# Key stores on GpSimd's queue, and four steps moved at the seam of two stages, in a graph attention kernel

## What is computed

```python
row_zero = x.sum(-1) == 0
q_exp = jnp.where(row_zero[..., None], 0.0, q[:, None, :])
self_feat = jnp.concatenate([x, q_exp], -1) @ W_self.T + b_self
output = self_feat
for d in range(2):
    A = adj if d == 0 else swapaxes(adj, 1, 2)       # [B, N, N, 11]
    A = A[:, :, :20, :]
    kv = self_feat[:, :20]                            # 20 keys for each of 128 batches
    qh, kh = heads(self_feat @ Wq[d].T + bq[d]), heads(kv @ Wk[d].T + bk[d])
    aff = einsum(qh, kh) / sqrt(dh) + mask(A) + (A @ w_bias + b_bias)
    w = softmax(aff, -1)
    output += heads_out(einsum(w, kv), Wout[d]) + bout[d]
out = x + relu(output)
```

## Time and profile before

| | us |
|---|---|
| median of 3 runs | 1888.92 |
| lowest and highest | 1884.96, 1889.0 |
| the profiled execution, whole time | 1889.68 |
| its span | 1887.9 |
| TensorE busy | 1790.1 (95%) |
| VectorE, ScalarE, GpSimd busy | 1117.5, 953.2, 773.0 |

### The profile page before, as it was taken

One profiled execution on the slowest core, in us unless ns is written; L12 is line 12 of the kernel. 1 busy time (PEld: TensorE's weight loads), 2 busy tenths in 40 slices (PEclk: granted clock), 3 DMA queues, 4 the chain that ended last, 5 costly groups with the idle time before them and its releaser, 6 DMA issues.

```text
span 1887.9 us, 45438 instructions
## 1 busy us (share of the span) xinstructions
PE 1790.1 (95%) x14792; PEld 1629.0 (86%) x14792; DVE 1117.5 (59%) x1879; ACT 953.2 (50%) x1655; POOL 773.0 (41%) x689
## 2 busy tenths in 40 slices
PE   8998778886999999999999999999999999999997
PEld 5898778885898999889899989999988989998886
DVE  2555455566666566666666666656666666666532
ACT  2333233333555555655555655555565555566543
POOL 0433333320344444444444444444444444444444
PEclk9998888997999999999999999999999999999999
DMA  7122222336555656555665655565755565565431
GB/s 213 37 77 77 72 71 76 82 101 138 142 148 150 185 147 173 148 147 154 166 170 148 165 147 149 146 185 134 189 149 147 148 168 169 147 172 148 122 99 61
DMA packets 291524, 258.16 MB, mean 137 GB/s; under 512 B 105968, under 2 KB 221936, under 8 KB 291312
## 3 DMA queue, kind: packets, MB, share of 16 engines
q1 hardware_dynamic: 287136, 255.46, 50.2%
q10 hardware_dynamic: 4176, 0.02, 0.1%
HBM read 199.25 MB, written 56.10 MB: 135 GB/s over the span
## 4 chain that ended last, share of the span: by engine, by line
PE 77%; issue 7%; SPq 7%; DVE 3%; POOL 3%; DMA 2%; ACT 1%; POOLq 0%; DVEq 0%; ACTq 0%
PE bank L1647 30%; PE bank L1662 20%; PE low_banks L1623 9%; PE bank L1683 9%; PE bank L1675 4%; SPq L663 4%; PE bank L1650 2%; PE bank L486 1%; POOL kv_prod L799 1%; SPq L70 1%; SPq L669 1%; DMA k_dram<-kv_kst 1%; PE bank L1691 1%; DVE kv_pt L717 1%; DVE kv_vt L756 1%
## 5 line engine op out<-in xcount | busy, mean ns | idle before, releaser
L1647 PE MATMUL bank<-kx,xt_main 128*128 128x160 f32 x4096 | 632.7, 303 | 0.0
L1647 PEld LDWEIGHTS bank<-kx,xt_main 128*128 128x128 f32 x4096 | 581.5, 192 | 6.0 <-issue 0.3
L1488 POOL TENSOR_TENSOR res<-res,xk 128x512 f32<-128x512 f32 x128 | 163.8, 1280 | 451.1 <-ACT res L1527 451.1
L1545 ACT ACTIVATE wtt<-bank 128x384 f32<-128x384 f32 (+1 forms) x256 | 109.6, 428 | 439.4 <-PE bank L1675 439.4
L1384 DVE TENSOR_TENSOR sc<-bank,masks 128x320 f32<-128x320 f32 x256 | 125.6, 491 | 341.9 <-PE bank L1650 340.1
L1532 ACT ACTIVATE kx<-low_banks 128x1920 f32<-128x1920 f32 (+5 forms) x201 | 306.2, 1524 | 43.1 <-PE low_banks L1623 43.0
L1470 POOL TENSOR_TENSOR sc<-sc,mx 128x640 f32<-128x640 f32 x128 | 160.0, 1271 | 310.5 <-DVE mx L1396 310.5
L1662 PE MATMUL bank<-ws_h,xh_main 128*128 128x512 f32 x512 | 217.7, 425 | 3.5 <-DVE res L1410 3.4
L1623 PE MATMUL low_banks<-key_tile,a_rows 32*128 32x160 f32 (+3 forms) x4288 | 202.5, 315 | 7.6 <-ACT kx L1532 4.0
L1662 PE MATMUL bank<-ws_l,xh_main 128*128 128x512 f32 x512 | 202.8, 396 | 0.0
L1662 PE MATMUL bank<-ws_h,xl_main 128*128 128x512 f32 x512 | 202.6, 396 | 0.0
(11 more groups left out here) (145 smaller groups left out, 3051.4 us busy)
## 6 DMA issues: line engine op xcount, KB each, us to landing
rows_main<-in_x SPq DMA_DIRECT2D x256, 128.0 KB, 4.6
xs<-in_x SPq DMA_DIRECT2D x64, 512.0 KB, 4.7
xk<-in_x SPq DMA_DIRECT2D x64, 512.0 KB, 3.7
res<-c_dram SPq DMA_DIRECT2D x64, 512.0 KB, 5.5
out<-res SPq DMA_DIRECT2D x128, 256.0 KB, 3.3
adj<-in_mask_BxSxSx_ik SPq DMA_DIRECT2D x32, 440.0 KB, 6.1
adj<-in_mask_BxSxSx_ik SPq DMA_DIRECT2D x128, 110.0 KB
vbd<-v_dram SPq DMA_DIRECT2D x768, 10.0 KB
```

Source lines behind the costliest of these rows:

```text
L1488: pool.tensor_tensor(res[:, p.par, b, :], res[:, p.par, b, :], xk[:, p.par, b, :], ALU.add).then_inc(res_ready, 1)
L1647: mm = nc.tensor.matmul(dst, xt[:, j, p.ring + b, :], kx[:, t.par, :, 2 * j:2 * j + 2, w * NG:w * NG + NG] .rearrange("p r c m -> p c r m" ...
```

## The change

1. The key stores leave SP. GpSimd issues the store of key p itself, inside `by_conditions`, after the wait for `kv_out` and ahead of the wait for `p_turned` and its product.
2. `late_loads` stands ahead of the value stores of half 7 (there are no key stores on SP now).
3. `early_turn` is cut in two. The turn of the first x pair goes to the end of half 6, behind `turn_constants(6)`; the mask's part (`early_mask`) stays where it was in half 7.
4. New `first_loads` on SP, between the value stores and the `z_dram` stores of half 7: the second edges and the second rows for sums, which the window loop's slot issued before.
5. The tile `zc` is cleared by GpSimd at the start of its window program, with a semaphore of its own, instead of by VectorE.

The diff, without the lines that only pass names along:

```diff
--- before.py
+++ after.py
@@ -646,22 +646,19 @@
                 for s in k_stored:
                     sp.wait_ge(s, 16 * C)
                 v["early_loads"](sp)
-            for p in range(NK):
-                if last and p == 2:
-
-                    sp.wait_ge(pe_feat, C * HALVES)
-                    sp.wait_ge(f_low, C * HALVES)
-                    v["late_loads"](sp)
-
-                sp.wait_ge(kv_out, 2 * NK * n + p + 1)
-                sp.dma_start(v["k_dram"][p, :, bass.ds(n * HB, HB), :],
-                             kst[:, p % 2, :].rearrange("p (b m) -> p b m", m=NG)).then_inc(k_stored[p % 2], 16)
+            if last:
+
+                sp.wait_ge(pe_feat, C * HALVES)
+                sp.wait_ge(f_low, C * HALVES)
+                v["late_loads"](sp)
             for m in range(NK):
                 d, c = m // C, m % C
                 sp.wait_ge(v_turned, NK * n + m + 1)
                 for k in range(NQ):
                     sp.dma_start(v["v_dram"][NQ * c + k, d, :, bass.ds(n * HB, HB), :],
                                  vt[Q * k:Q * k + NG, m % 4]).then_inc(v_stored[m % 4], 16)
+            if last:
+                v["first_loads"](sp)
             sp.wait_ge(z_turned, n + 1)
             for r in range(NQ):
                 for e in range(2):
...
@@ -742,11 +739,7 @@
             if not tail:
                 turn_x(blk + 1, n + 2, par)
             if last:
-
-                dve.wait_ge(pe_feat, C * HALVES)
-                dve.wait_ge(x_low, C * HALVES)
-                dve.wait_ge(f_low, C * HALVES)
-                v["early_turn"](dve)
+                v["early_mask"](dve)
             for m in range(NK):
 
                 dve.wait_ge(kv_out, 2 * NK * n + NK + m + 1)
...
@@ -757,6 +750,11 @@
                 if m < 2:
                     constant_sums(n, 6 + m)
             turn_constants(n)
+            if tail and not last:
+
+                dve.wait_ge(pe_feat, C * HALVES)
+                dve.wait_ge(x_low, C * HALVES)
+                v["early_turn"](dve)
 
         nonzero(0, 0)
         dve.wait_ge(v["ct_out"], 1)
...
@@ -794,6 +792,8 @@
         def by_conditions(n, p):
 
             pool.wait_ge(kv_out, 2 * NK * n + p + 1)
+            pool.dma_start(v["k_dram"][p, :, bass.ds(n * HB, HB), :],
+                           kst[:, p % 2, :].rearrange("p (b m) -> p b m", m=NG)).then_inc(k_stored[p % 2], 16)
             if due(NK * n + p - 1):
                 pool.wait_ge(p_turned, NK * n + p - 1)
             pool.tensor_tensor(prod[:, p % 2, 1, :].rearrange("p (b m) -> p b m", m=NG),
...
@@ -1057,6 +1057,7 @@
     edge_consts = sem("edge_consts")
     set_once = sem("set_once")
     cleared = sem("cleared")
+    zc_cleared = sem("zc_cleared")
     x_turned = sem("x_turned")
     x_high = sem("x_high")
     x_low = sem("x_low")
...
@@ -1271,9 +1272,18 @@
     def early_turn(dve):
         dve.wait_ge(rows_loaded[0], 16 * NQ)
         turn_pair(dve, Pair(0, 0), range(C))
+
+    def early_mask(dve):
         dve.wait_ge(edge_consts, 32)
         count_and_weigh(dve, 0, 0)
         total_and_mask(dve, 0, 0)
+
+    def first_loads(sp):
+
+        sp.wait_ge(bias_sum[0], 1)
+        load_edges(sp, 1, 0)
+        sp.wait_ge(summed, 2)
+        load_sum_rows(sp, Pair(0, 1))
 
     def load_constants(sp, p):
 
...
@@ -1304,7 +1314,7 @@
                 if t.back(4).real():
                     sp.wait_ge(pe_s, scored(t.back(1), 3))
                 elif t.n == 0:
-                    sp.wait_ge(set_once, 2)
+                    sp.wait_ge(zc_cleared, 1)
                 load_constants(sp, t)
             if has_window(n) and due(t.n + 1):
 
...
@@ -1324,8 +1334,9 @@
                 g = edge_group(t.back(-1))
                 if has_edges(g) and due(g):
 
-                    sp.wait_ge(bias_sum[0], g)
-                    load_edges(sp, g, 0)
+                    if not isinstance(g, int) or g > 1:
+                        sp.wait_ge(bias_sum[0], g)
+                        load_edges(sp, g, 0)
             if done.real():
                 store(done, 0)
             if due4.real():
...
@@ -1346,7 +1357,7 @@
                     sp.wait_ge(res_ready, 2 * (due4.n - 1))
                 sp.dma_start(xk[:, due4.par],
                              v["x"][bass.ds(2 * due4.n, 2)].rearrange("b n f -> n b f")).then_inc(xk_loaded[due4.par], 16)
-            if n.real() and due(n.n):
+            if n.real() and due(n.n - 1):
 
                 sp.wait_ge(summed, 2 * n.n)
                 load_sum_rows(sp, n)
...
@@ -1363,9 +1374,8 @@
             sp.wait_ge(s, 32 * (PAIRS // 2))
 
     def vector_program(dve):
-        nc.vector.memset(zc[:].bitcast(F32), 0.0).then_inc(set_once, 1)
         nc.vector.memset(nzm[:], 0.0).then_inc(set_once, 1)
-        dve.wait_ge(set_once, 2)
+        dve.wait_ge(set_once, 1)
         for b in range(2):
             for o in (0, 2):
                 nc.vector.memset(nzm[:, b::2, ZK * b + o:ZK * b + o + 1], 1.0).then_inc(set_once, 1)
...
@@ -1443,7 +1453,7 @@
             if has_edges(g) and (due(g) or t.c % 2):
                 total_and_mask(dve, g, t.c % 2)
 
-        dve.wait_ge(set_once, 6)
+        dve.wait_ge(set_once, 5)
         slots(dve, slot, -1)
 
     def s_bank(t, a):
...
@@ -1451,6 +1461,8 @@
         return bank[4 + n][:, 0:2 * UN]
 
     def gpsimd_program(pool):
+        pool.wait_ge(v["kv_out"], 4 * DIRS * C * v["KBLOCKS"])
+        pool.memset(zc[:].bitcast(F32), 0.0).then_inc(zc_cleared, 1)
         for s in v["k_stored"]:
             pool.wait_ge(s, 16 * DIRS * C * v["KBLOCKS"])
         for s in v["v_stored"]:
```

4 lines of the change are left out of this document (2 added, 2 removed).

## The result

The changed kernel takes 1820.38 us (median of 4 runs, 1817.72 to 1824.19) where the kernel before takes 1887.42 in the same comparison: a ratio of 0.9647, with a 95% interval of 0.9623 to 0.9672. That is 67.0 us or 3.5% faster, at the forecast of 1816 within 4.4 us and inside its range. The profiled execution took 1818.22 us, its span is 1816.2, and the span before was 1887.9: 71.7 us less.

The account below looks back on a forecast made before the run. Key stores queued behind SP's other transfers held the halves above TensorE's pace. Halves at 36.5 us give 58.7 and the seam 14.5, together 73.2 us off the profiled 1889.68; with the median 0.76 lower, 1816 us, range 1811 to 1845.

Parts of the forecast that it names:

- g: Time GpSimd takes to issue one key store; unknown before, chosen near 0.97 us.
- S: Time from a key store's issue on GpSimd to its landing, taken as g + 1.47 us.
- the ring: Half's chain of keys, GpSimd's stores and landings: 25.15 + 3(g + S), 35.4 us, hidden under TensorE's 36.26 by 0.9.
- 2g + 5.45: Time from key 0 of a half until store 2 goes out, behind two issues, two products and the conditions.
- S + 2.4: One step from a key store's issue to the next, for stores 3 to 5, each waiting for a landing.
- g + 12.5: From store 5 to the next half's key 0: issue, product, x turn, then value transposes.
- the sum's term: Seam path through the second rows for sums: out at 35.05, first scores at 44.3 us, a gain of 15.3.
- A: The forecast itself: halves at TensorE's pace, up to 37 us, giving 1813 to 1819 us; chance 0.62.
- B: Halves: the ring through GpSimd takes over, 39.8 us a half and 1839 us at g = 1.7; chance 0.25.
- C: Halves: only SP's issue time is saved, 2.7 us a half, giving 1856 us; chance 0.04.
- D: Halves: slower, GpSimd's issue as dear as ScalarE's longest, 3.98 us; 53.4 us a half, 1934 us; chance 0.05.
- E: Seam: another input of the first scores comes as late as before; only 58.7 us gained, 1830 us; chance 0.04.

Follow-up runs that it names:

- The stores alone: Changed kernel with only the key stores moved to GpSimd; x turn, first loads and clearing of zc put back as before: 1824.18 us, ratio 0.9670.
- The store behind the product: Changed kernel with GpSimd issuing each key store after its own product of the same tile instead of ahead of it: 1829.71 us, ratio 0.9699.
- three stores for one: Changed kernel with GpSimd issuing two extra scratch stores ahead of each key store, ScalarE waiting for all three: 1879.67 us, ratio 0.9956.

## Why the prediction was right, point by point

**The bound.** Right. What held the halves was the place of the key stores behind SyncE's other transfers. The stores alone gave 58.2 us in the halves, and eight more issues a half on SyncE cost 0.3 of their 3.2 us there. The forecast took TensorE's pace from half 0, which ran without gaps, so the 11 us that the clock gave back are in its sum, though it does not name them.

**The halves: right in the sum, by two errors.** Forecast 36.5, measured 36.61 a half, though not even: 35.19 to 38.65. The price of GpSimd's issue was too high:

```profile
L795 POOL DMA_DIRECT2D k_dram<-kv_kst x64: 580/580/710, 81.0 to 351.5; - x64
```

g is 0.58 us at the least and at the median, not 0.97. The landing was 2.3 at the median (2.1 to 6.5), where S = g + 1.47 with g = 0.97 had given 2.44. With these, 25.15 + 3(g + S) is 33.8, and the halves should all have been hidden under TensorE's 36.26. Half 3, of 38.65 us, shows what the ring really was. Its first piece, key 0 to store 2, was 9.02 us, where 2g + 5.45 gives 6.61; in halves 0 to 2 and 4 to 6 it was 6.91 to 7.91. The step that failed is the conditions' place in the row:

```profile
195.95 3.09 POOL L776 TENSOR_TENSOR kv_rc<-kv_nz,kv_cbb 128x320 f32<-128x320 bf16 x4 [2.20 <-DVE kv_cbb L676]
```

GpSimd's conditions wait for VectorE, which the row of before that I had used did not the earlier trace rows, and store 2 stands behind them. That row is of half 1; in halves 2 to 5 of the kernel before the same instruction waited 0.62 to 1.96 us for VectorE. The next steps were 4.98, 4.82 and 5.15 us, the S + 2.4 of the prediction with an S of 2.4 to 2.8. From store 5 to the next key 0 were 14.68, where g + 12.5 gives 13.08; in five of the other six halves it was 13.11 to 13.14, as worked out. Behind both long pieces of half 3 stand SyncE's value stores, for which VectorE waits before it can use a slot of `vt` again:

```profile
193.99 0.71 DVE L749 STREAM_TRANSPOSE kv_vt<-kv_vst 128x512 f32<-128x512 f32 x1 [2.57 <-DMA v_dram<-kv_vt]
...
227.12 0.71 DVE L749 STREAM_TRANSPOSE kv_vt<-kv_vst 128x512 f32<-128x512 f32 x1 [1.08 <-DMA v_dram<-kv_vt]
```

The first is the last value transpose of half 2, and VectorE makes the conditions' inputs only behind it, from 195.22; the second is the last but one of half 3, just ahead of key 0 of half 4. So the ring passes TensorE's pace in half 3, and in halves 4 and 5, of 35.19 and 35.68, it is 0.7 to 1.2 us below it.

TensorE lost nothing by this. Its last matmuls for key 0 of halves 3 and 4 are

```profile
188.53 0.31 PE L933 MATMUL low_banks<-kv_fh,wkv_l 128*128 128x320 f32 x1
...
224.90 0.31 PE L933 MATMUL low_banks<-kv_fh,wkv_l 128*128 128x320 f32 x1
```

36.37 us apart, and it is the same, within 0.01, from each half to the next from half 1 to half 7; in the window from 116 to 336 us TensorE is busy for 220.00 of 220.00. The 38.65 are ScalarE falling behind by 2.3 us more, which the six banks took up. So the 1.9 us that the kernel with ScalarE's stores has less in its halves (254.42 for 256.29) are nearly all ScalarE's lag of 1.8 us at key 0 of half 7, and not time of TensorE. TensorE's pace of 36.26 a half was right to 0.1.

**ScalarE's wait: a miss that cost the halves nothing.** The wait for landings fell from 130.0 us to 81.3 in 28 waits, not to under 25. Such a row is in each step of the ring:

```profile
206.40 0.53 ACT L853 ACTIVATE kv_kst<-low_banks,bk_s 128x320 f32<-128x320 f32 x1 [3.34 <-DMA k_dram<-kv_kst]
```

I had counted only what a landing would add beyond the step. But in a ring in which ScalarE works 1.5 us of a step of 4.8, it waits some 3.3 for whatever is last, and the landing became that in place of the product. TensorE waited 0.6 us for it in all, against 52.1 before, so the wait was on the side with slack. The wait said how near the ring was, not what it cost. What a shorter ring is worth shows at the seam: with ScalarE's own stores halves and seam together are 296.4 us and not 300.6.

**SyncE.** Right. It stands idle from 211.48, the end of its x loads, to 220.45, 9 us, within half 3, and 9.7 to 14.3 us in each of halves 1, 2 and 4 to 6.

**The seam: the number right, partly by luck.** Forecast 44.3, measured 44.31. From key 0 of half 7: VectorE began its sums at 5.6 (forecast 5.0), the mask at 16.36 (16.6), the value stores at 21.05 (21.3), the sum rows went out at 34.85 (35.05). The mask was forecast to wait for its edges. They were issued at 11.75 and not at 10.5, but landed 4.0 us later and not 6.1, at 15.8, and the mask's start was the end of VectorE's sums, which had been put at 15.3: two errors that cancel to 0.2 us. The z stores landed 3.30 us behind their last issue, not 1.6, so at 41.7 and not 40.0:

```profile
374.52 3.30 DMA z_dram<-kv_zt
```

The constants' loads then landed 2.5 behind their issue at 377.89, near the short end that was allowed, and they, not the sum rows, were the last for the first scores, by the 0.41 us of the row above. The chain of the sum rows ended at 43.9; the forecast's 9.26 from their issue to the first scores was itself 0.2 too long, since the first scores of before start at 453.82 in the timeline and not at 454.03. So the sum's term was the second to last, and the two paths ended within half a microsecond of each other. The gain is 15.1, where 14.5 was taken and 9.8 to 15.3 was the range. Of it 8.7 come with the stores alone.

**The early turn, and the clearing.** The prediction had the turn's 2.1 us hidden. The kernel that undoes it is 2.8 us longer in the seam and 0.9 to 2.3 in the median, with a late landing of the edges in the trace, so this stays open, as told above. Clearing the tile was said to cost nothing on GpSimd, and it doesn't; that it would have cost 1.3 to 1.8 us if left on VectorE was not worked out.

**The sum.** Forecast 73.2 less in the span, measured 71.7: halves 57.95 for 58.7, seam 15.1 for 14.5, less 1.3 before and behind, which is spread. The medians differ by 67.0: the profiled execution of the kernel before took 2.3 us more than its median, that of the changed kernel 2.2 less.

**The rivals.** A held. B is real but lies farther out: at g = 0.58 the ring is just below TensorE's pace in most halves. The store behind the product costs 1.1 us a half, and three stores for one, 1.66 us of issue, cost 7.9 and give 1879.67. For C, see above: neither the 1856 nor its cause. The Trainium skill's rule (DMA: Bandwidth & Descriptors, "Issuing engines are not separate DMA queues"), that several issuing engines save only the sequencer's time, does not describe this kernel: the issue time saved was 2.7 us a half, and the gain was 8.3. What counted was which store stood behind which on one queue. The estimate for the landing that was worked out from the Trainium skill (the same page, "Anatomy of one DMA"), 2.4 us, agrees with the 2.3 measured. D did not come near. E did not happen: another input, the constants, did come last, but only by 0.4 us.

## What to carry to other kernels

When a small, urgent transfer waits behind large ones that nobody waits for, move it to a queue whose earlier instructions are done by the time it is ready, and put it directly behind the instruction that makes its data. Price the new queue's ring, not only its issue: everything the new engine does ahead of the store in program order, with what that waits for, is now part of the path. If the producing engine can issue the store itself, as ScalarE did here for 0.34 us, try it: of the four places measured here it was the fastest.

## What the runs showed of the hardware

- One issue of 160 KB by GpSimd over 128 rows took 0.58 us at the median (0.71 at most), by ScalarE 0.34; the stores landed 2.3 and 2.0 us from issue at the median.
- Three such stores in a row on GpSimd's queue had landed 3.6 to 5.9 us after the first issue in half 4 of that kernel, where one needs 2.3 to 2.8 in halves 3 to 5 of the changed one.
- SyncE's eight z stores took 3.2 to 4.9 us to issue, in different halves of one execution of the changed kernel.
- The first edges of the mask, 440 KB, landed in anything from 3.9 to 6.8 us from their issue, in nearly the same place of nearly the same program.
- TensorE's 1500 or so matmuls of halves 1 to 6 took 231.0 us of busy time with gaps between them and 220.0 without, at mean granted clocks of 0.91 and 1.00.
